# Edges in a cyclic buffer of ten pieces, one transfer at every second step, and preparation's buffers moved into places of the masks

## The reference

```python
Wh = (h @ W.T).reshape(n, K, OUT_DIM).transpose(1, 0, 2)          # K = 4 heads
e = leaky_relu(score_src + score_dst, 0.2)                        # per head, 8192 x 8192
e = where(adj == 0, -inf, e)
alpha = softmax(e, axis=-1)
h_prime = einsum('kij,kjd->kid', alpha, Wh)
return layernorm(x + h_prime.transpose(1, 0, 2).reshape(n, K * OUT_DIM))
```

## Time and profile before

| what | before |
|---|---|
| median of 3 runs | 1407.2 us |
| the runs | 1402.2, 1407.2, 1410.06 us |
| the profiled execution | 1408.21 us |
| its span, first to last instruction | 1406.2 us |
| mean granted TensorE clock | 0.971 of full speed |
| busy share of DVE, ACT, POOL, PE | 96%, 90%, 89%, 85% |
| DMA of the edges: 256 transfers, us from issue to landing (median) | 5.2 |

### The profile page before, as it was taken

How to read it: one execution, slowest core, us unless ns; L and a number is a source line. 1 busy time by engine, 2 the same in 40 slices (tenths; PEclk the granted TensorE clock), 3 DMA queues, 4 the chain that set the end, 5 groups by cost and what they waited for, 6 DMA issues and landing times.

```text
span 1406.2 us, 77028 instructions
## 1 busy us (share of the span) xinstructions
PE 1196.3 (85%) x35173; PEld 1159.3 (82%) x35173; DVE 1351.8 (96%) x1599; ACT 1269.4 (90%) x1344; POOL 1247.3 (89%) x1316
## 2 busy tenths in 40 slices
PE   7047788889899988989988999988898889999886
PEld 7046678889898888889888988988898889889886
DVE  7979999999999999999999999999999999999998
ACT  3799989999999989999999999999999999999652
POOL 1699779999899989999998999999999999999762
PEclk9569999999999999999999999999999999999998
DMA  8216455766666575666766676666756666676640
GB/s 167 63 32 55 40 78 56 85 76 63 90 63 95 56 99 56 65 90 67 100 58 91 57 91 73 64 90 63 97 54 95 62 71 83 63 81 64 69 42 25
DMA packets 55838, 101.61 MB, mean 72 GB/s; under 512 B 5720, under 2 KB 18392, under 8 KB 55512
## 3 DMA queue, kind: packets, MB, share of 16 engines
q0 software_dynamic: 36864, 67.13, 53.1%
q1 hardware_dynamic: 18648, 29.56, 6.6%
HBM read 293.67 MB, written 4.33 MB: 212 GB/s over the span
## 4 chain that ended last, share of the span: by engine, by line
PE 50%; DVE 20%; issue 17%; POOL 6%; ACT 5%; DMA 1%; DVEq 0%; SPq 0%; ACTq 0%; POOLq 0%
PE bank L796 45%; DVE rest L636 8%; POOL kept L354 5%; PE bank L782 5%; DVE kept L627 5%; ACT kept L460 4%; DVE late L647 1%; DVE bank L577 1%; DVE late L649 1%; DMA edge<-in_adj 1%; DVE G L541 1%; DVE kept L616 1%; DVE kept L543 1%; DVE late L588 1%; DVE F L591 1%
## 5 line engine op out<-in xcount | busy, mean ns | idle before, releaser
L460 ACT ACTIVATE kept<-s_two,sd 128x1024 uint8<-128x1024 f32 (+1 forms) x1152 | 1184.2, 1118 | 78.3 <-PE bank L796 40.9
L354 POOL TENSOR_SCALAR kept<-s_two,sd 128x1024 uint8<-128x1024 f32 (+1 forms) x896 | 969.7, 1096 | 75.1 <-DVE rest L636 39.0
L636 DVE TENSOR_TENSOR rest<-kept,bank 128x1024 int32<-128x1024 int32 x512 | 599.9, 1212 | 20.1 <-PE bank L796 19.5
L796 PE MATMUL bank<-G,kept 128*128 128x66 f16 x16384 | 554.4, 193 | 74.6 <-issue 40.4
L627 DVE TENSOR_TENSOR kept<-bank,kept 128x1024 int32<-128x1024 int32 x512 | 600.8, 1214 | 10.4 <-ACT kept L460 6.1
L796 PE MATMUL bank<-F,rest 128*128 128x66 f16 x16384 | 562.5, 194 | 49.4 <-issue 30.1
L796 PEld LDWEIGHTS bank<-G,kept 128*128 128x128 fp8e4 x16384 | 525.1, 97 | 88.1 <-issue 45.0
L796 PEld LDWEIGHTS bank<-F,rest 128*128 128x128 fp8e4 x16384 | 522.6, 98 | 68.0 <-issue 34.5
L782 PE MATMUL bank<-identb,edge 128*128 128x128 bf16 x2048 | 158.8, 221 | 51.6 <-ACT G L457 43.5
L350 POOL DMA_DIRECT2D edge<-in_adj x256 | 151.0, 590 | 15.4 <-DMA kept<-in_x 15.3
L782 PEld LDWEIGHTS bank<-identb,edge 128*128 128x128 bf16 x2048 | 120.0, 98 | 53.3 <-ACT G L457 43.7
(11 more groups left out here) (76 smaller groups left out, 338.4 us busy)
## 6 DMA issues: line engine op xcount, KB each, us to landing
edge<-in_adj POOLq DMA_DIRECT2D x256, 256.0 KB, 5.2
s_two<-sT_scratch SPq DMA_DIRECT2D x30, 512.0 KB, 4.7
kept<-in_x SPq DMA_DIRECT2D x16, 256.0 KB, 5.8
y<-in_x SPq DMA_DIRECT2D x16, 256.0 KB, 4.7
out<-y SPq DMA_DIRECT2D x16, 256.0 KB, 3.0
s_two<-sT_scratch SPq DMA_DIRECT2D x2, 256.0 KB, 3.7
y<-sT_scratch SPq DMA_DIRECT2D x1, 256.0 KB, 3.6
late<-sT_scratch SPq DMA_DIRECT2D x1, 256.0 KB, 4.8
```

The lines of the kernel that those rows point to most:

```text
L354: return nc.gpsimd.tensor_scalar(out, scores, STEEP, d_steep[:, j, h:h + 1], ALU.mult, ALU.add)
L460: return nc.scalar.activation(out, scores, ACT.Sigmoid, scale=STEEP, bias=d_steep[:, j, h:h + 1])
L636: nc.vector.tensor_tensor(rest[:, k % NL], kept[:, r, both(q, q)[0]], edgeT[q % NT], ALU.bitwise_xor).then_inc(rest_set, 1)
L796: last = nc.tensor.matmul(acc[k][:, col:col + BC], matrix[:, u, b * P:(b + 1) * P, e], values[:, q * IB + u * E + e, h].rearrange("p s c - ...
```

## The change

The buffer of edges becomes a ring of ten pieces instead of two chunks of four. Each piece has a semaphore of its own. The first ten pieces are issued in the preparation where eight were; from step 9 on POOL issues one piece after its tiles of every odd step, piece 10 + (k - 9) / 2, so one per quad instead of four in four neighbouring steps out of eight. Piece n still waits until PE has transposed the whole chunk of the piece that lay there before. PE waits for four semaphores, one after the other, at every fourth quad. The larger buffer (20 KB instead of 16 KB in each partition) is paid for by `late`, which shrinks from 2304 to 1056 words: `xT`, `left` and `s_rows` now lie in places 14 to 21 of ring 1 of `kept`, which the masks of group 0 reach later, and the second buffer of `s_first` moves forward in `late`. The order of the preparation's instructions and all their other waits stay as they are.

```diff
-    NC = 2
+    NP = 10
+    PIECE_LAG = 9
     CHUNK = CP * E * P
-    EDGE_UNITS = (1, 2, 3, 4)
...
-        edge = sb("edge", [P, NC, IB, CHUNK], i8)
+        edge = sb("edge", [P, NP, CHUNK], i8)
...
-        late = sb("late", [P, max(2 * CHUNKS * HC, NX * ROWS + 2 * P)], fp32)
-        xT = late[:, 0:NX * ROWS].rearrange("p (n r) -> p n r", n=NX)
+        late = sb("late", [P, 2 * CHUNKS * HC], fp32)
+        spare = kept[:, 1, :, :].rearrange("p n w -> p (n w)").bitcast(fp32)
+        LEFT_AT, XT_AT, ROWS_AT = 14 * WORDS, 17 * WORDS, 21 * WORDS
+        xT = spare[:, XT_AT:XT_AT + NX * ROWS].rearrange("p (n r) -> p n r", n=NX)
...
-        FIRST_AT = JB * HEADS + NU * TJ * HEADS * HC
+        FIRST_AT = JB * HEADS
...
-        edge_loaded = [sem(f"edge_loaded{n}") for n in range(NC)]
+        edge_loaded = [sem(f"edge_loaded{n}") for n in range(NP)]
...
-            def load_edges(c, b):
-                if c >= NC and b == 0:
-                    pool.wait_ge(transposed, (c - NC + 1) * CQ)
-                nc.gpsimd.dma_start(edge[:, c % NC, b], adj_v[c // (PAIRS // CP), c % (PAIRS // CP), :, b // E, b % E]
-                                    ).then_inc(edge_loaded[c % NC], 16)
+            def load_edges(n):
+                c, b = n // IB, n % IB
+                if n >= NP:
+                    pool.wait_ge(transposed, ((n - NP) // IB + 1) * CQ)
+                nc.gpsimd.dma_start(edge[:, n % NP], adj_v[c // (PAIRS // CP), c % (PAIRS // CP), :, b // E, b % E]
+                                    ).then_inc(edge_loaded[n % NP], 16)
...
-            for c in range(NC):
-                for b in range(IB):
-                    load_edges(c, b)
+            for n in range(NP):
+                load_edges(n)
...
-                    if t % CP in EDGE_UNITS and NC <= k // CP + 1 < GROUPS * PAIRS // CP:
-                        load_edges(k // CP + 1, EDGE_UNITS.index(t % CP))
+                    if k >= PIECE_LAG and (k - PIECE_LAG) % 2 == 0 and NP + (k - PIECE_LAG) // 2 < GROUPS * PAIRS // CP * IB:
+                        load_edges(NP + (k - PIECE_LAG) // 2)
...
-                    pe.wait_ge(edge_loaded[c % NC], 16 * IB * (c // NC + 1))
+                    for n in range(c * IB, c * IB + IB):
+                        pe.wait_ge(edge_loaded[n % NP], 16 * (n // NP + 1))
```

More of the change, by code:

```diff
@@ L117, in gat_layernorm @@
         y = sb("y", [P, IB, D_IN], fp32)
-        edge16 = edge[:, :, :, :].bitcast(bf16)
+        edge16 = edge[:, :, :].bitcast(bf16)
         kept_u8, kept_f8 = (kept[:, :, :, :].bitcast(dt).rearrange("p r n (u i e) -> p r n u i e", u=U, e=E) for dt in (u8, fp8))
@@ L138, in gat_layernorm @@
         sigma = sb("sigma", [P, 2], fp32)
-        late = sb("late", [P, max(2 * CHUNKS * HC, NX * ROWS + 2 * P)], fp32)
-        xT = late[:, 0:NX * ROWS].rearrange("p (n r) -> p n r", n=NX)
+        late = sb("late", [P, 2 * CHUNKS * HC], fp32)
+        spare = kept[:, 1, :, :].rearrange("p n w -> p (n w)").bitcast(fp32)
+        LEFT_AT, XT_AT, ROWS_AT = 14 * WORDS, 17 * WORDS, 21 * WORDS
+        xT = spare[:, XT_AT:XT_AT + NX * ROWS].rearrange("p (n r) -> p n r", n=NX)
         zs = late[:, 0:JB * HEADS].rearrange("p (j h) -> p j h", h=HEADS)
-        left = late[:, JB * HEADS:JB * HEADS + NU * TJ * HEADS * HC].rearrange("p (n j h c) -> p n j h c", n=NU, h=HEADS, c=HC)
-        s_rows = late[:, NX * ROWS:NX * ROWS + 2 * P].rearrange("p (n r) -> p n r", n=2)
-        FIRST_AT = JB * HEADS + NU * TJ * HEADS * HC
+        left = spare[:, LEFT_AT:LEFT_AT + NU * TJ * HEADS * HC].rearrange("p (n j h c) -> p n j h c", n=NU, h=HEADS, c=HC)
+        s_rows = spare[:, ROWS_AT:ROWS_AT + 2 * P].rearrange("p (n r) -> p n r", n=2)
+        FIRST_AT = JB * HEADS
+        assert NU * TJ * HEADS * HC <= XT_AT - LEFT_AT and NX * ROWS <= ROWS_AT - XT_AT and FIRST_AT + ROWS <= 2 * CHUNKS * HC
         s_first = (y[:, :, :].rearrange("p b f -> p (b f)"), late[:, FIRST_AT:FIRST_AT + ROWS])
@@ L782, in transpose_edges @@
                         last = nc.tensor.transpose(edgeT16[q % NT][:, (u * IB + b) * P:(u * IB + b + 1) * P],
-                                                   edge16[:, c % NC, b, at:at + P], identb[:, :])
+                                                   edge16[:, (c * IB + b) % NP, at:at + P], identb[:, :])
                 last.then_inc(transposed, 1)
```

## The result

| what | before | after |
|---|---|---|
| median of six runs each, side by side | 1407.93 us | 1445.82 us |
| lowest and highest | 1401.05 to 1410.06 | 1440.17 to 1447.56 |
| ratio, 95% interval | | 1.0285, 1.0258 to 1.0313 |
| span of the profiled execution | 1406.2 us | 1443.8 us |

The changed kernel is 2.9% slower, some 38 us. The forecast was 1409 with a range up to 1420, so both the number and the range were wrong. The lines of the code moved by three or four: `take_step` is L630 (L627 before), `take_rest` L639 (L636), PE's transposes L786 (L782), PE's matmuls L800 (L796), POOL's masks L358 (L354), its issues of edges L354 (L350).

The account below looks back on a forecast made before the run. DVE's own work plus its little waiting was taken to bound the kernel. 1408.2 + 1.05 + 0.95 - 0.1 = 1410.1, less 1.0 for the median, gave 1409 us; range 1393 to 1420.

Parts of the forecast that it names:

- What bounds the kernel, and why PE stops: Whole run: DVE's work plus waits; PE stops because instruction refills wait for edge transfers; at most 19.5 us to gain.
- The regular beat: Steady part: as many refills should meet a transfer, only places change; taken as 0, between -19.5 and +22 us.
- The slower rival: Steady part: stalls fall in quads where DVE has no other work; +11 or +22 us, 1420 or 1431; chance 0.22.
- train: Steady part: some seven neighbouring quads with stalls, 4.6 us together, once in a group, as refills slide through transfers.
- the wandering: Steady part: refills do not come a whole number of times in a group, so the train wanders; no size given.
- POOL's count argument: Steady part: by any step no more transfers are issued than now, so POOL's masks and closing parts are not later; nothing.
- Two more transfers in flight: Preparation: edges make the second load of s_first land 1.9 us later, 0.85 us of it free; +1.05 us (0 to 2.45).
- My sign for a confirmed term: Preparation: POOL's first mask near 49.1 us instead of 47.2 would confirm the term for Two more transfers in flight.
- the turn of the queues: Preparation: s_first waiting to the edges' end makes the sum 1.4 us higher; the skill's packet-by-packet turns, about 1 us lower.
- Four waits on PE: PE's queue: three more 51 ns waits at 62 chunks, 9.5 us, a tenth of it taken; +0.95 us (0 to 9.5).
- the issues hidden under POOL's wait: Preparation: two more issues add 1.1 us to POOL, under its 13.49 us wait for DVE; nothing.
- PE's wait for edges gone: Steady part: pieces arrive earlier, so PE's wait for edges, 1.2 us in the run, vanishes; -0.1 us (-1.2 to 0).

Follow-up runs that it names:

- halved pair: The changed kernel and the kernel before, each loading only half of every piece after the first ten or eight: ratios 0.9905 (1389.43 us) and 0.9857 (1384.71 us).
- the even steps: The changed kernel with each issue of a transfer moved from the odd to the even step, first at step 10: 1502.3 us, ratio 1.0711.
- pairs: The changed kernel with transfers begun after two neighbouring steps out of four (t % 4 = 1 and 2): 1442.74 us, ratio 1.0274.
- tiles 3, 9, 12, 14: The changed kernel's ring with eight pieces issued first and a chunk's four pieces begun after these of POOL's 14 tiles: 1425.39 us, ratio 1.0166.
- the kernel with two late pieces: The changed kernel, but POOL begins pieces 8 and 9 only after its wait for s_first: 1447.41 us, ratio 1.0319.
- the halved kernel with the ring: The changed kernel, loading only the first half of each piece from the eleventh on: 1389.43 us, ratio 0.9905.

## Why the prediction was wrong, step by step

- **What bounds the kernel, and why PE stops: right.** DVE's work and its waits are the time; halved transfers returned 19.7 us to the kernel before, and 18.1 of the 19.5 us of the earlier trace rows went with them.
- **The regular beat, taken at 0: wrong, and the largest error.** I said that as many transfers meet as many refills, and let the refill slide through the transfers by 0.4 us a quad. The slide exists only while no refill is held. A held one starts when its transfer ends, whatever its own beat was, so the next one's fate hangs on the next interval: 91% are held again at 4.8 to 6.7 us, 16% under 4.2. Refills that stall went from 72 of 235 to 96 of 228, and those that follow straight on another from 22 to 48. The beat itself came unevenly, too: 3.9, 5.0 and 6.0 us between issues, by the tiles between them. The material was in the earlier trace rows: the refill 4.6 us after the issue; I didn't follow it to the next refill. The old places, 2.8 us apart (3.9 where a closing part lies between) and then over 9 us, lie outside the harmful interval, 3 of 219 apart.
- **The slower rival: right in kind, too low in chance (0.22) and in price.** It said that PE's spare of 0.22 us a quad is too small for a train, 11 to 22 us; `take_rest` gave 15.8. That this lies in its bounds is partly luck: its train slid through the transfers once in a group with 62 us of stops as before, and what ran were stalls that bring on the next, with 89.0 us. Against it I held "the wandering", which the held refill abolishes. And it left out the end of a group: PE, late there, lets DVE wait for the closed banks, 11.1 us that no step of mine priced.
- **POOL's count argument: true, and beside the point.** The issues were not more and no mask or closing part kept DVE waiting. But I took the closing parts as free for the transfers, too; the parts at t = 7 and 19 and the power at t = 28 stretch intervals of three tiles from 3.9 us to between 4.9 and 5.4.
- **Two more transfers in flight, +1.05 (0 to 2.45): a wrong step.** I moved the landing of the loads of `s_first` and let them be issued at 42.20 us as before. I went past SP's queue without the two stores in front of them, which also share the engines: 7.8 us instead of 2.9. The price is 4.0 us. My sign for a confirmed term, 49.1 us for POOL's first mask, was passed by 2.75 us. On the turn of the queues, where I set the rows against the Trainium skill (page "DMA: Bandwidth & Descriptors", section "Queues, rings and completion order"): the page's turns are by packet, and packets there hold several descriptors. A refill that is held until the transfer is through, but for less time when the transfer is halved, fits turns by packets as large as a transfer's share of an engine. The profile's row of the queue counts 144 records to a transfer (31680 for 220 in the earlier trace rows), nine for each of 16 engines. If these are the page's descriptors, of which it has some 9 to 17 in a packet, my reading was wrong and not the rule; no run here measured a packet, so this stays open.
- **Four waits on PE, +0.95: too many instructions.** PE's wait instructions at the edges in after, by line:

```profile
L780 PEldq EVENT_SEMAPHORE  x65: 51/51/51, 35.0 to 1401.8; - x65
```

```profile
L782 PEldq EVENT_SEMAPHORE  x63: 51/51/51, 102.4 to 1402.0; - x63
```

  They are 128 where I expected about 250 and the earlier trace rows had 63, all of 51 ns: 65 times 51 ns, 3.3 us over the run, a third of the 9.5 that was my upper end; the sum had 0.95. I took each wait for an instruction of its own. In the trace of after each of these instructions names two semaphores, and the weight load behind them a third.
- **Right as said:** the issues hidden under POOL's wait, PE's wait for edges gone, no wait of DVE for POOL after 83 us, nothing for moved buffers that any row shows (1 to 3 us of the halved pair's difference stay unassigned).
- **Not priced at all:** DVE's three small operations, +0.5 us a group, from POOL's masks that now lie across them. "Same work, other time" was taken to be free; it is not where two engines hold each other up.

Open at the end: what tips the even steps; why the stops are longer in pairs and with tiles 3, 9, 12, 14; what part of PE's lateness is its lower clock after a stop; POOL's 11 us in the kernel with two late pieces; and how much of the 7.2 us of DVE would come back by moving masks alone.

## What to carry to other kernels

Where an engine's instruction refills wait behind large transfers, spacing the transfers evenly is no smoothing: a held refill is set anew by the transfer, so ask what the next transfer does to the next refill. Here only bursts of four with pauses of over 9 us stayed level; a beat near the time between refills, pairs and other spreads cost 1.7 to 7%. Fewer bytes to a transfer helped, but cutting it into more issues cost the issuing engine more than it gave. When transfers are begun earlier, follow every other DMA that is in flight at that time, the small stores ahead of a load too, and what waits for their landing. When one engine is late by a little everywhere, price the ends of the groups as well as the steady part, since the lag is paid where its last result is read.

## What the runs showed of the hardware that was not expected

- A held refill starts about 4.5 us after the issue of the transfer (4.2 to 4.8 for eight in ten), and PE resumes 2.2 to 2.6 us after it starts (486.65 to 488.95 us, 491.65 to 494.07, and at every stop over 0.3 us in after).
- PE's granted clock falls to 0.50 of full speed for 3.4 us at a time, in before and after behind stops of 1.6 to 2.5 us: five times in after, three in before, fifteen with transfers at even steps, never in the halved kernel with the ring.
- One step's shift of the same transfers is worth some 56 us: 1445.82 us at odd steps, 1502.3 at even ones.
- Two stores that land after 2.9 us with eight edge transfers ahead take 7.8 us with ten.
- POOL's issue of a transfer takes 556 ns for 64 rows and, in the preparation, 562 for 128 (4.50 us for eight).
- A transfer of half the bytes from each row holds the engines for some two thirds of the time (39.8% for 224 transfers against 59.7% for 213).
- A DVE operation of 170 ns on SBUF alone takes up to 569 ns when it begins inside a mask of POOL, and ends with it.
